# A transformer kernel: first self-attention in one block with float32r parts, further expert turns of 64 rows, exponents head by head, and another order of two loads

## The chip, the core and the metric

The kernel runs on one core of one Trainium2 chip. The measure is the device time of the whole program in microseconds; the median of several runs counts.

## What is computed

The reference takes x, 8 sequences of 64 rows of 512 (512 rows in all), and ctx, 8 times 1601 rows of 384, all float32. Six stages follow each other, each of them `x = x + stage(layernorm(x))`:

```python
x = x + _L0_xattn_ref(_layernorm(x), ctx_768, ...)   # 8 heads over the context
x = x + _L0_attn_ref(_layernorm(x), Wq, Wk, Wv)      # one head of 512, rotated q and k, mask tril(k=1)
x = x + _L0_ffn_ref(_layernorm(x), ...)              # 8 gated experts, 2 chosen per row, hidden 512
x = x + _L1_xattn_ref(_layernorm(x), ctx_768, ...)   # top-32 attention, FiLM, long convolution, feed-forward
x = x + _L1_attn_ref(_layernorm(x), Q, K, V, W)      # 16 heads of 64, causal
x = x + _L1_ffn_ref(_layernorm(x), ...)              # 8 GELU experts, 2 chosen per row, hidden 2048, a shared layer
```

The softmax of the two self-attentions is exact, and an expert works only for the rows that chose it.

## The kernel before

The 512 rows lie as four tiles of 128 (TT = 4), the 512 features as four chunks of 128 (KC = 4). A stage is one or several blocks; within a block each engine has its own program, and all order between engines is written out by hand with semaphores. At the end of a block all engines wait for each other. Loads go through SP's queue unless said otherwise. PE writes sums to PSUM, eight banks of 512 columns.

**First self-attention** (`self_attention_L0`, L610). A block holds only SP's six loads (L638 to L641). Then `norm_stage` (L133 to L167) normalises x on DVE and POOL, transposes it on PE and copies it to xt on ACT. Then comes the block of the work: PE multiplies Wq and Wk with xt in full precision (L667), four banks at a time, and K waits until DVE has multiplied Q by the tables (L698) and so freed the banks. The rotated halves are joined at L700 and L701. The values follow (L673), then the scores of each row tile (L680), mask (L704), maximum (L708), exponent with its sum (L726), reciprocal, a pass that divides (L714), the transposes (L685), the weighted values (L688) and the addition to x (L717). SP writes zeros to the two scratch tensors `sent` and `back` meanwhile (L651).

**Experts** (`experts`, L798), used for both mixtures. Each row's two chosen experts are found, and its normalised row is sent by POOL's indirect DMAs to `sent`, sorted by expert, each expert's rows padded to a multiple of 128. Then for each expert there is one fresh turn of 128 rows, and further turns if it has more (`turns`: a branch on the count, and a loop over k = 1 to 3 with a branch inside, on every engine). In a turn PE computes the hidden rows (`up`, L998) in NG groups of four chunks of 128, ACT applies bias and GELU for the second experts (L1252) and writes h; PE sums y from h and w2 (`down`, L985). In between it transposes the next 128 rows (L980), which ACT loads to e_xr (L1226; for the first time SP, L897, behind the weights of two experts) and copies to xg (L1230). DVE copies y (L1153) and ACT stores it to `back` (L1234). The last `down` of a turn stands after the first `up` of the next, and in a fresh turn a drain (L1014) follows it. It frees w2 for SP's load two experts on (L776 to L780). At the end POOL gathers each row's two results.

**End of the top-k attention** (`top_attention`). DVE picks the 32 best scores in passes of 8, ACT takes exponents, POOL subtracts (L2149), PE forms the mean attention (L1950) and weighs the context (L1965) for each of 8 batches. For the last batch PE first multiplies the value weights with the seven batches that are done (L1996); they come with ten small loads (`load_few`, L1769 to L1776), which SP issues after the filter weights (`load_film`, 4 MB, L1764), and these after the last scores.

**Second self-attention** (`self_attention_L1`). Projections with float32r: each float32 operand is cut into a high and a low part (ACT casts, L1457; DVE subtracts, L1510), and three products replace one in full precision (L1384). Then 16 units of 4 heads and 128 rows each. Per unit: scores on PE (L1405), on DVE scale and mask (L1529), maximum (L1532), subtraction (L1534), on ACT the exponent (L1479), on DVE sum (L1540), reciprocal, multiplication (L1544), on PE the transposes (L1414), on ACT a copy to pt (L1489), on PE the weighted values (L1425), on ACT a copy to yt (L1496). Every four units PE projects (L1434) and DVE adds to x (L1503).

## Time and profile before

| | us |
|---|---|
| Median of 3 runs | 1928.32 |
| The runs | 1927.71, 1928.32, 1939.1 |
| The profiled execution in all | 1944.16 |
| Its span (first to last instruction) | 1942.3 |

The page of the profile gives busy time by engine and line; the timeline gives operations in order with the engine's idle time before them and who ended it, in square brackets. An idle time matters only where PE, or whoever ends last, has it. The granted clock of TensorE was 0.944 of full speed on average. Matmuls in float32 stand as two records each, float32r ones and transposes as one.

### The profile page before, as it was taken

What the parts mean: (1) busy time and instruction counts of PE and PEld (TensorE: products, weight loads), DVE (VectorE), ACT (ScalarE), POOL (GpSimd) and SP (SyncE); (2) the same over time, 40 slices, a digit from 0 to 9 for tenths busy, and PEclk for the clock granted to TensorE, in tenths of its full rate; (3) what the DMA queues carried; (4) which work ended last, traced back from release to release, by engine and by line L of the source; (5) the groups of instructions that cost most, each with busy time, mean ns of one, the idle gap of its engine ahead of it and who ended that gap; (6) DMA issues with size and microseconds to landing.
All of it is one profiled execution on the core that took longest, in us unless ns stands there. A gap on an engine that the chain in (4) does not pass through costs nothing. (4 is left out here: it accounts for less than half of the span.)

```text
span 1942.3 us, 23742 instructions
## 1 busy us (share of the span) xinstructions
PE 1754.5 (90%) x8998; PEld 1350.7 (70%) x8998; DVE 981.5 (51%) x1490; ACT 573.9 (30%) x988; POOL 341.6 (18%) x294
## 2 busy tenths in 40 slices
PE   7899999999987889958999969797988899999994
PEld 3899999999953677723656547386775567777762
DVE  1667787686822434438899976644347310000003
ACT  4354443544410111113344412142433121111110
POOL 0432233312200010023454521100000010000002
PEclk9999999999998899978898989899989899999997
DMA  3332213322107346463444330700200565455802
GB/s 123 102 102 69 85 52 102 102 65 89 39 28 261 134 167 219 169 202 132 155 163 155 125 127 1 276 1 1 88 1 1 192 256 190 175 211 204 346 27 71
DMA packets 109978, 243.09 MB, mean 125 GB/s; under 512 B 13824, under 2 KB 43024, under 8 KB 105248
## 3 DMA queue, kind: packets, MB, share of 16 engines
q1 hardware_dynamic: 100672, 220.97, 32.1%
q10 hardware_dynamic: 6624, 12.06, 1.8%
q0 software_dynamic: 2560, 8.39, 1.3%
q8 instruction: 81, 1.33, 0.3%
q14 instruction: 41, 0.34, 0.1%
HBM read 221.48 MB, written 19.92 MB: 124 GB/s over the span
## 5 line engine op out<-in xcount | busy, mean ns | idle before, releaser
L998 PEld LDWEIGHTS e_ps<-e_xg,e_w 128*128 128x128 f32 x2304 | 269.0, 193 | 48.0 <-issue 45.6
L998 PE MATMUL e_ps<-e_xg,e_w 128*128 128x128 f32 x2304 | 272.4, 277 | 8.4 <-issue 4.4
L371 PE MATMUL x_s_ps<-x_cxt,x_qs 128*128 128x400 f32 (+1 forms) x1152 | 244.3, 357 | 10.0 <-POOL x_qs L344 5.9
L397 PE MATMUL x_o_ps<-x_cx,x_pt 128*128 128x386 f32 (+1 forms) x1248 | 230.3, 343 | 0.0
L985 PE MATMUL e_ps<-e_w,xt 128*128 128x512 f32 x480 | 221.0, 600 | 0.9 <-ACT xt L1252 0.6
L397 PEld LDWEIGHTS x_o_ps<-x_cx,x_pt 128*128 128x128 f32 (+1 forms) x1248 | 220.6, 190 | 1.4
L371 PEld LDWEIGHTS x_s_ps<-x_cxt,x_qs 128*128 128x128 f32 x1152 | 205.5, 191 | 11.2 <-issue 11.1
L1153 DVE COPY e_y<-e_ps 128x512 f32<-128x512 f32 x24 | 16.5, 688 | 340.1 <-PE e_ps L985 340.1
L1936 PE MATMUL x_s_ps<-x_cxt,x_qs 128*128 128x512 f32 (+1 forms) x384 | 142.7, 528 | 7.8 <-POOL x_qs L2132 5.8
L985 PEld LDWEIGHTS e_ps<-e_w,xt 128*128 128x128 f32 x480 | 86.6, 192 | 84.2 <-issue 82.2
L1252 ACT ACTIVATE xt<-e_ps,e_b 128x128 f32<-128x128 f32 x192 | 54.8, 369 | 282.1 <-PE e_ps L998 276.1
L1936 PEld LDWEIGHTS x_s_ps<-x_cxt,x_qs 128*128 128x128 f32 x384 | 68.6, 196 | 84.9 <-issue 79.0
L447 DVE TENSOR_TENSOR x_pt<-x_t_ps,x_pt 128x512 fp32r<-128x512 f32 (+1 forms) x128 | 74.7, 587 | 91.4 <-ACT x_pt L537 91.1
L537 ACT CAST x_pt<-x_t_ps 128x512 fp32r<-128x512 f32 (+1 forms) x128 | 64.6, 506 | 158.4 <-PE x_t_ps L383 157.4
L1284 POOL DMA_INDIRECT e_w<-back,m_row x16 | 16.5, 1032 | 497.1 <-ACTq L1270 492.8
L2203 DVE MAX8 x_best<-x_left 128x8 f32<-128x1601 f32 x48 | 87.8, 1829 | 1.7
L2205 DVE MATCH_REPLACE8 x_left<-x_best,x_left 128x1601 f32<-128x1601 f32 x48 | 86.9, 1811 | 0.0
L383 PE MATMUL x_t_ps<-ident,x_pr 128*128 128x128 f32 (+1 forms) x416 | 66.6, 274 | 2.0 <-DVE x_pt L447 2.0
L438 DVE TENSOR_REDUCE x_nmost<-x_s_ps 128x1 f32<-128x1600 f32 x32 | 58.4, 1825 | 14.4 <-PE x_s_ps L371 14.4
L513 ACT ACTIVATE x_pr<-x_s_ps,x_nmax 128x1600 f32<-128x1600 f32 x32 | 51.2, 1600 | 47.0 <-DVE x_nmax L440 47.0
L332 POOL TENSOR_TENSOR x_cx<-x,x_cx 128x1536 fp32r<-128x1536 f32 (+1 forms) x16 | 34.0, 2124 | 154.1 <-PE x_o_ps L397 144.8
L1950 PE MATMUL x_a_ps<-x_mean,x_sc 128*128 128x64 f32 (+1 forms) x416 | 56.3, 306 | 4.2 <-POOL x_sc L2149 4.2
(369 smaller groups left out, 2565.1 us busy)
## 6 DMA issues: line engine op xcount, KB each, us to landing
e_w<-in_L_ffn_W SPq DMA_DIRECT2D x16, 4096.0 KB, 16.3
x_cxt<-in_ctxT SPq DMA_DIRECT2D x8, 2401.5 KB, 8.6
x_cx<-in_ctx SPq DMA_DIRECT2D x8, 2304.0 KB
e_w<-in_L_ffn_gate_up_proj SPq DMA_DIRECT2D x8, 2048.0 KB, 11.1
x_stage<-in_ctxT SPq DMA_DIRECT2D x16, 768.0 KB, 4.4
x_stage<-in_ctx SPq DMA_DIRECT2D x16, 768.0 KB, 5.8
e_w<-in_L_ffn_down_proj SPq DMA_DIRECT2D x8, 1024.0 KB, 9.2
ff_w<-in_L_xattn_W SPq DMA_DIRECT2D x2, 4096.0 KB
```

The lines of the kernel that those rows point to most:

```text
L371: last = nc.tensor.matmul(s_ps[:, n, 0:b - a], qs[:, u % 2, p, c, :], cxt[:, q, c, a:b], start=(m + c == 0), stop=(m + c == len(PARTS) + C ...
L383: last = nc.tensor.transpose(t_ps[0:rows, g % 2, (t - a) * P:(t - a + 1) * P], pr[:, t * P:t * P + rows], ident[:, :])
L397: last = nc.tensor.matmul(o_ps[:, 0:WIDE], pt[0:rows, p, t, :], cx[0:rows, q, t, :], start=(t + m == 0), stop=(t + m == KT - 1 + len(PARTS ...
L438: nc.vector.reduce_max(nmost[:, u % 2:u % 2 + 1], s_ps[:, :, 0:400], AXIS.XY, negate=True).then_inc(most_ready, 1)
L447: nc.vector.tensor_tensor(pt[0:rows, 1, a:b, :], t_ps[0:rows, g % 2, 0:(b - a) * P].rearrange("p (t n) -> p t n", n=P), pt[0:rows, 0, a:b, ...
L537: nc.scalar.copy(pt[0:rows, 0, a:b, :], t_ps[0:rows, g % 2, 0:(b - a) * P].rearrange("p (t n) -> p t n", n=P)).then_inc(pth_ready, 1)
L985: last = nc.tensor.matmul(y_ps, h[:, c, :], w2[:, e % PAIR, c, :], start=(c == 0), stop=(c == HC - 1))
L998: last = nc.tensor.matmul(u_ps[:, g % 2, a * PER + n, :], w1[:, e % PAIR, m, a * hidden + c * P:a * hidden + (c + 1) * P], xg[:, m, :], st ...
L1936: last = nc.tensor.matmul(s_ps[:, lo:hi], qs[:, r, c, :], cxt[:, j, c, lo:hi], start=(c == 0), stop=(c == CC - 1))
L1950: last = nc.tensor.matmul(a_ps[0:rows, t * S:(t + 1) * S], sc[:, j, r, t * P:t * P + rows], mean[:, r, :], start=(r == 0), stop=(r == HALV ...
L2203: V.max(best[:, r, 8 * n:8 * n + 8], source).then_inc(steps, 1)
L2205: V.match_replace(left[:, r, :], best[:, r, 8 * n:8 * n + 8], source, TAKEN).then_inc(steps, 1)
```

## The change

Four parts. **A**: the first self-attention becomes one block: SP's loads, the norm and the work together. Wq, Wk, Wv and x are cut into float32r parts, and each projection is three products (`PARTS`); Q and K have four banks each. The weight tiles are taken in the order 0, 2, 1, 3, and DVE rotates in four turns of half a matrix. Two value tiles stand before the scores, two after. The pass that divides is gone: the reciprocal goes into the last addition. **B**: in the second experts a further turn has 64 rows (`MORE`): rows are the stationary side, the weights the moving one; GELU is applied on rows, the result transposed back. The bias is added by DVE from rows that two more loads per expert bring. A fresh turn ends with its own `down` groups and has no drain. In both mixtures the loop (third turn and later) now stands before the second turn. **C**: in the second self-attention ACT subtracts the maximum as its bias, head by head, and sums. **D**: `load_few` goes before `load_film`. The setting of lines that both versions share is left out here.

```diff
             @block.sync
             def _(sp):
-                for dst, name, s in ((wq, "L0_attn_Wq", in_q), (wk, "L0_attn_Wk", in_k), (wv, "L0_attn_Wv", in_v)):
-                    sp.dma_start(dst[:, :, :], w[name].rearrange("(c p) n -> p c n", p=P)).then_inc(s, 16)
-                sp.dma_start(cos[:, :, :], w["rope_cos"].rearrange("(c p) n -> p c n", p=P)).then_inc(in_tab, 16)
-                sp.dma_start(sin[:, :, :], w["rope_sin"].rearrange("(c p) n -> p c n", p=P)).then_inc(in_tab, 16)
-                sp.dma_start(mask[:, :], w["mask_L0"]).then_inc(in_tab, 16)
-
...
-            @block.sync
-            def _(sp):
+                for slot, name, s in ((0, "L0_attn_Wq", in_q), (1, "L0_attn_Wk", in_k)):
+                    sp.dma_start(wqk[:, slot, :, :], w[name].rearrange("(c p) n -> p c n", p=P)).then_inc(s, 16)
+                for a, name in enumerate(("rope_cos", "rope_sin")):
+                    sp.dma_start(tables[:, a, :, :], w[name].rearrange("(c p) n -> p c n", p=P)).then_inc(in_tab, 16)
...
+                for n in range(2 * KC):
+                    bank = (n // KC) * KC + ORDER[n % KC]
+                    for p, q in PARTS:
+                        if n == 0:
+                            pe.wait_ge((xh_ready, xl_ready)[q], TT)
+                        pe.wait_ge((wh_ready, wl_ready)[p], n + 1)
                         for c in range(KC):
...
+                            last = nc.tensor.matmul(ps[:, bank, :], part(n, p)[:, c, :], xs[:, q, c, :],
+                                                    start=(c == 0 and p + q == 0), stop=(c == KC - 1 and q == 1))
...
+                def value(t):
+                    for p, q in PARTS:
+                        pe.wait_ge((vh_ready, vl_ready)[q], KC)
+                        for c in range(KC):
+                            last = nc.tensor.matmul(ps[:, t, :], xs[:, p, c, t * P:(t + 1) * P], vs[:, q, c, :],
+                                                    start=(c == 0 and p + q == 0), stop=(c == KC - 1 and q == 1))
+                    last.then_inc(v_ready, 1)
+
+                pe.wait_ge(rot_ready, 4)
+                value(0)
+                value(1)
+                pe.wait_ge(rot_ready, 8)
                 for t in range(TT):
                     for c in range(KC):
...
+                        last = nc.tensor.matmul(ps[:, KC + t, 0:P], rot[:, 0, c, t * P:(t + 1) * P], rot[:, 1, c, t * P:(t + 1) * P],
                                                 start=(c == 0), stop=(c == KC - 1))
                     last.then_inc(s_ready, 1)
+                value(2)
+                value(3)
                 for t in range(TT):
-                    pe.wait_ge(norm_ready, t + 1)
-                    nc.tensor.transpose(qk_ps[:, t, 0:P], pr[:, t, :], ident[:, :]).then_inc(t_ready, 1)
+                    pe.wait_ge(exp_ready, t + 1)
+                    nc.tensor.transpose(ps[:, KC + t, P:2 * P], pr[:, t, :], ident[:, :]).then_inc(p_ready, 1)
...
+                norm.statistics(dve)
+                norm.rows(dve)
+                for t in range(TT):
+                    weight_low(t)
+                    dve.wait_ge(xh_ready, t + 1)
+                    here = xs[:, :, :, t * P:(t + 1) * P]
+                    V.tensor_tensor(here[:, 1, :, :], tps[:, t, :, :], here[:, 0, :, :].bitcast(F32), ALU.subtract).then_inc(xl_ready, 1)
+                for n in range(KC, 2 * KC):
+                    weight_low(n)
+                for c in range(KC):
+                    dve.wait_ge(vh_ready, c + 1)
+                    V.tensor_tensor(vs[:, 1, c, :], wv[:, c, :], vs[:, 0, c, :].bitcast(F32), ALU.subtract).then_inc(vl_ready, 1)
+                dve.wait_ge(in_tab, 32)
...
+                    for j in range(HALF):
+                        turn = a * HALF + j
+                        even, odd = ps[:, a * KC + j, :], ps[:, a * KC + HALF + j, :]
+                        cos, sin = tables[:, 0, j, :], tables[:, 1, j, :]
+                        dve.wait_ge(qk_ready, 2 * turn + 2)
+                        dve.wait_ge(rot_ready, 2 * turn)
+                        for n, (source, table) in enumerate(((even, cos), (odd, sin), (even, sin), (odd, cos))):
+                            V.tensor_tensor(tmp[:, n, :], source, table, ALU.mult).then_inc(prod_ready, 1)
+                        dve.wait_ge(prod_ready, 4 * turn + 2)
+                        V.tensor_tensor(rot[:, a, j, :], tmp[:, 0, :], tmp[:, 1, :], ALU.subtract).then_inc(rot_ready, 1)
+                        dve.wait_ge(prod_ready, 4 * turn + 4)
+                        V.tensor_tensor(rot[:, a, HALF + j, :], tmp[:, 2, :], tmp[:, 3, :], ALU.add).then_inc(rot_ready, 1)
...
                     dve.wait_ge(y_ready, t + 1)
-                    nc.vector.tensor_tensor(x[:, t, :], x[:, t, :], r_ps[:, t, :], ALU.add)
+                    V.scalar_tensor_tensor(x[:, t, :], ps[:, t, :], red[:, 2, t:t + 1], x[:, t, :], ALU.mult, ALU.add)
...
+                def weight_high(n):
+                    if n % KC == 0:
+                        act.wait_ge((in_q, in_k)[n // KC], 16)
+                    nc.scalar.copy(part(n, 0), tile(n)).then_inc(wh_ready, 1)
+
                 for t in range(TT):
+                    weight_high(t)
+                    act.wait_ge(t_ready, t + 1)
+                    nc.scalar.copy(xs[:, 0, :, t * P:(t + 1) * P], tps[:, t, :, :]).then_inc(xh_ready, 1)
+                for n in range(KC, 2 * KC):
...
                 for t in range(TT):
                     act.wait_ge(max_ready, t + 1)
                     nc.scalar.activation(pr[:, t, :], pr[:, t, :], ACT.Exp, bias=red[:, 0, t:t + 1],
...
+                    if t == 1:
+                        copy_value(3)
+                    act.wait_ge(p_ready, t + 1)
+                    nc.scalar.copy(pt[:, t, :], ps[:, KC + t, P:2 * P]).then_inc(pt_ready, 1)
 
...
+                sp.dma_start(self.b1_rows[half * S:(half + 1) * S, e % PAIR, :, :], bcast(self.up_rows[e, half], S)
+                             ).then_inc(self.rows_in[e % PAIR], 16)
         sp.dma_start(self.w2[:, e % PAIR, :, :], self.down_w[e].rearrange("(c p) n -> p c n", p=P)).then_inc(self.w2_in[e % PAIR], 16)
 
...
-                            engine.reg_add(register, register, 1)
+                    with engine.Fori(BLOCKS + 1, TOK // MORE) as k:
+                        with engine.If(k * MORE < tokens):
+                            one_more(e)
+                    one_more(e)
             return engine.snap(register, min_val=1, max_val=TURNS)
 
         with nc.Block() as block:
@@ -985,27 +1082,29 @@
...
+                def fresh_turn(e, t):
+                    pe.wait_ge(w1_in[e % PAIR], (e // PAIR + 1) * 16)
+                    pe.wait_ge(xg_ready, t + 1)
+                    one = up(e, t, 0)
+                    if e:
+                        one.then_inc(w1_free, 1)
+                    else:
+                        pe.wait_ge(b_ready, TT)
+                    one = up(e, t, 1)
+                    if e:
+                        one.then_inc(w2_free, 1)
+                        pe.wait_ge(y_ready, t)
+                    pe.wait_ge(w2_in[e % PAIR], (e // PAIR + 1) * 16)
+                    for g in range(NG):
+                        pe.wait_ge(h_ready, t * NG + (g + 1))
+                        last = down(e, g)
+                        if g + 2 < NG:
+                            up(e, t, g + 2)
+                        if g + 3 == NG:
+                            pe.wait_ge(x_in, (t + 1) * 16)
...
+                def more_turn(e, t, n):
+                    pe.wait_ge(xg_ready, t + 1)
+                    for p in range(2):
+                        for m in range(KC):
+                            for half in range(2):
+                                lo = half * S
+                                last = nc.tensor.matmul(ur_ps[lo:lo + S, p, :], xg[:, m, 0:S],
+                                                        w1[:, e % PAIR, m, (2 * p + half) * 512:(2 * p + half + 1) * 512],
+                                                        start=(m == 0), stop=(m == KC - 1))
+                        last.then_inc(up_ready, NG // 2)
+                    for p in range(2):
+                        pe.wait_ge(smooth, n * 2 + (p + 1))
+                        for c in range(KC):
+                            last = nc.tensor.transpose(ht_ps[:, p, c * P:(c + 1) * P], hr[:, p, c * P:(c + 1) * P], core.ident[:, :])
+                        last.then_inc(turned, 1)
+                        if p == 0:
+                            pe.wait_ge(x_in, (t + 1) * 16)
+                            turn_rows()
+                    pe.wait_ge(y_ready, t)
+                    for p in range(2):
+                        pe.wait_ge(h_ready, t * NG + (p + 1) * (NG // 2))
+                        for c in range(KC):
+                            for half in range(2):
+                                for q in range(2):
+                                    last = nc.tensor.matmul(y_ps[q * S:(q + 1) * S, 0:D // 2], h[:, p * KC + c, half * S:(half + 1) * S],
+                                                            w2[:, e % PAIR, (2 * p + half) * KC + c, q * (D // 2):(q + 1) * (D // 2)],
+                                                            start=(p + c + half == 0), stop=(p == 1 and c == KC - 1 and half == 1))
+                    last.then_inc(down_ready, 1)
+
+                if gated:
...
+                def more_turn(e, t, n):
+                    dve.wait_ge(rows_in[e % PAIR], (e // PAIR + 1) * 32)
+                    for p in range(2):
+                        dve.wait_ge(up_ready, t * NG + (p + 1) * (NG // 2))
+                        V.tensor_tensor(hr[:, p, :], ur_ps[:, p, :], weights.b1_rows[:, e % PAIR, p, :], ALU.add).then_inc(added, 1)
+                    for p in range(2):
+                        dve.wait_ge(turned, n * 2 + (p + 1))
+                        V.tensor_copy(h[:, p * KC:(p + 1) * KC, :], ht_ps[:, p, :].rearrange("p (c n) -> p c n", n=P)).then_inc(h_ready, NG // 2)
+                    dve.wait_ge(down_ready, t + 1)
+                    dve.wait_ge(y_out, (t + 1) * 16)
+                    V.tensor_copy(y[:, 0:D // 2], y_ps[:, 0:D // 2]).then_inc(y_ready, 1)
+
...
+                def more_turn(e, t, n, row):
+                    act.wait_ge(x_ready, t + 1)
+                    load_rows(row + 1)
+                    for p in range(2):
+                        act.wait_ge(added, n * 2 + (p + 1))
+                        nc.scalar.activation(hr[:, p, :], hr[:, p, :], ACT.Gelu).then_inc(smooth, 1)
+                    copy_rows(t + 1)
+                    act.wait_ge(y_ready, t + 1)
+                    act.dma_start(back[bass.ds(row * MORE, S), :].rearrange("r (h n) -> h r n", h=2), y[:, 0:D // 2]).then_inc(y_out, 16)
 
                 act.sem_inc(y_out, 16)
                 copy_rows(0, first_ps)
...
                     nc.scalar.copy(v[:, t, half * 512:(half + 1) * 512], ps[:, n % 8, :]).then_inc(p_used, 1)
                 def exponent(u):
-                    act.wait_ge(low_ready, u + 1)
-                    nc.scalar.activation(pr[:, u % AHEAD, :, :], pr[:, u % AHEAD, :, :], ACT.Exp).then_inc(exp_ready, 1)
+                    act.wait_ge(max_ready, u + 1)
+                    for k in range(G):
+                        one = pr[:, u % AHEAD, k, :]
+                        last = nc.scalar.activation(one, one, ACT.Exp, bias=red[:, u % AHEAD, 0, k:k + 1],
+                                                    accum_out=red[:, u % AHEAD, 1, k:k + 1])
+                    last.then_inc(exp_ready, 1)
 
...
                                                    mask[:, :].unsqueeze(1).broadcast_to([P, G, P]), ALU.mult, ALU.add).then_inc(sm_ready, 1)
                     dve.wait_ge(sm_ready, u + 1)
-                    nc.vector.reduce_max(red[:, k, 0, :], pr[:, k, :, :], AXIS.X).then_inc(max_ready, 1)
-                    dve.wait_ge(max_ready, u + 1)
-                    nc.vector.tensor_tensor(pr[:, k, :, :], pr[:, k, :, :], red[:, k, 0, :].unsqueeze(2).broadcast_to([P, G, P]),
-                                            ALU.subtract).then_inc(low_ready, 1)
+                    nc.vector.reduce_max(red[:, k, 0, :], pr[:, k, :, :], AXIS.X, negate=True).then_inc(max_ready, 1)
 
                 def normal(u):
                     k = u % AHEAD
                     dve.wait_ge(exp_ready, u + 1)
-                    nc.vector.reduce_sum(red[:, k, 1, :], pr[:, k, :, :], AXIS.X).then_inc(sum_ready, 1)
-                    dve.wait_ge(sum_ready, u + 1)
                     nc.vector.reciprocal(red[:, k, 2, :], red[:, k, 1, :]).then_inc(inv_ready, 1)
                     dve.wait_ge(inv_ready, u + 1)
                     nc.vector.tensor_tensor(pr[:, k, :, :], pr[:, k, :, :], red[:, k, 2, :].unsqueeze(2).broadcast_to([P, G, P]),
...
                     if b + 3 == B:
+                        sp.wait_ge(qs_ready, B * HALVES)
+                        mix.load_few(sp)
                         sp.wait_ge(s_ready, B * HALVES)
                         mix.load_film(sp)
-                        sp.wait_ge(qs_ready, B * HALVES)
-                        mix.load_few(sp)
```

## Rows read from the trace of the kernel before

**Rows 1.** The page: busy by engine; chain by engine; one costliest group.

```profile
PE 1754.5 (90%) x8998; PEld 1350.7 (70%) x8998; DVE 981.5 (51%) x1490; ACT 573.9 (30%) x988; POOL 341.6 (18%) x294
...
PE 18%; DMA 1%; DVE 1%; POOL 0%; issue 0%; DVEq 0%; ACT 0%; ACTq 0%
...
L1153 DVE COPY e_y<-e_ps 128x512 f32<-128x512 f32 x24 | 16.5, 688 | 340.1 <-PE e_ps L985 340.1
```

**Rows 2.** Timeline (start us, us, operation), PE in the second experts' turns.

```profile
1615.61 0.60 PE L980 MATMUL e_ps<-ident,e_xr 128*128 128x128 f32 x4
...
1623.06 3.60 PE L985 MATMUL e_ps<-e_w,xt 128*128 128x512 f32 x8
...
1644.58 0.60 PE L980 MATMUL e_ps<-ident,e_xr 128*128 128x128 f32 x4
...
1673.04 0.60 PE L980 MATMUL e_ps<-ident,e_xr 128*128 128x128 f32 x4
```

**Rows 3.** Timeline of the first self-attention.

```profile
582.75 0.37 SPq L638 DMA_DIRECT2D s_wq<-in_L_attn_Wq  x1
...
588.17 3.22 PE L156 MATMUL n_tps<-ident 128*128 128x128 f32 x14 [7.68 <-PEq L634]
...
596.15 13.97 PE L667 MATMUL s_qk_ps<-xt,s_wq 128*128 128x512 f32 x32 [1.84 <-PEq L54]
...
614.99 16.72 PE L667 MATMUL s_qk_ps<-xt,s_wk 128*128 128x512 f32 x32 [4.87 <-DVE s_tmp L698]
...
651.65 1.12 PE L685 MATMUL s_qk_ps<-ident,s_pr 128*128 128x128 f32 x4 [2.64 <-DVE s_pr L714]
...
657.29 0.69 DVE L717 TENSOR_TENSOR x<-x,s_r_ps 128x512 f32<-128x512 f32 x1 [0.17 <-PE s_r_ps L688]
```

**Rows 4.** Timeline of the second self-attention's loop: two projections.

```profile
1463.48 7.13 PE L1434 MATMUL s_ps<-s_wz,s_yt 128*128 128x512 f32 x16
...
1484.24 7.13 PE L1434 MATMUL s_ps<-s_wz,s_yt 128*128 128x512 f32 x16
```

**Rows 5.** Groups of instructions: busy us, mean ns, idle before; records that price the parts.

```profile
L1384 PE MATMUL s_ps<-s_xs,s_ws 128*128 128x512 f32 x192 | 45.3, 399 | 3.2 <-DVE s_ws L1510 3.2
...
L1534 DVE TENSOR_TENSOR s_pr<-s_pr,s_red 128x512 f32<-128x512 f32 x16 | 11.1, 692 | 0.6
...
L1540 DVE TENSOR_REDUCE s_red<-s_pr 128x4 f32<-128x512 f32 x16 | 10.9, 678 | 0.0
...
L1479 ACT ACTIVATE s_pr<-s_pr 128x512 f32<-128x512 f32 x16 | 10.1, 629 | 4.0 <-DVE s_pr L1534 3.9
...
L726 ACT ACTIVATE s_pr<-s_pr,s_red 128x128 f32<-128x128 f32 x4 | 1.6, 390 | 3.5 <-DVE s_red L708 3.5
```

**Rows 6.** Timeline of the end of the top-k attention.

```profile
1135.55 11.15 PE L1996 MATMUL x_s_ps<-x_ct,x_qp 128*128 128x448 f32 x24 [9.44 <-DMA x_qp<-in_dft_inverse]
...
1141.11 3.02 POOL L2149 TENSOR_TENSOR x_sc<-x_sc,x_left 128x1601 f32<-128x1601 f32 x1
...
1146.54 5.70 PE L1950 MATMUL x_a_ps<-x_mean,x_sc 128*128 128x64 f32 x52
```

**Rows 7.** Timeline: matmuls with 64 stationary columns, from three stages.

```profile
1153.29 4.73 PE L1965 MATMUL x_e_ps<-x_cx,x_at 128*64 128x384 f32 x26 [1.05 <-ACT x_at L2066]
...
1219.50 1.93 PE L2377 MATMUL mx_ps<-mx_spec,x_qp 128*64 128x512 f32 x4 [1.34 <-DVE mx_spec L2405]
...
1515.03 1.83 PE L1425 MATMUL s_ps<-s_pt,s_v 128*64 128x128 f32 x16
```

**Rows 8.** Timeline: the second experts' first turned rows and what follows.

```profile
1585.39 0.66 PE L980 MATMUL e_ps<-ident,e_xr 128*128 128x128 f32 x4 [2.38 <-DMA e_xr<-sent]
1585.89 5.29 PE L985 MATMUL e_ps<-e_w,xt 128*128 128x512 f32 x8
```

**Rows 9.** Busy by engine in two stretches; then granted clock, DMA share, GB/s.

```profile
616.00:620.00 4.00, 4.00 (x6) 1.66 (x5) 1.24 (x2) 0.00 (x0) 0.00 (x0) 0.50 0.91 338
1620.00:1640.00 20.00, 19.74 (x115) 14.30 (x115) 0.69 (x1) 3.43 (x12) 0.00 (x0) 1.00 0.95 362
```

## What the change will do to the time

> **What bounds the kernel.** I read the page first. Over a span of 1942.3 us PE is busy 90% and DVE 51%; the named part of the chain that ended last is 18% PE, almost all of it the second experts [rows 1]. So a microsecond counts where PE works longer or waits, and the other engines count only where PE waits for them. Then I read the four places that the diff touches in the timeline, each for the operation that ends last there.
>
> In the second experts PE sets the pace and nothing else does. The 24 copies of y are 24 turns, 12 for each block of experts [rows 1]. From one group of turned rows to the next a turn takes 28.97 us (1615.61 to 1644.58), or 28.46 us (1644.58 to 1673.04) where no drain stands in it [rows 2].
>
> In the first self-attention PE works on full-precision matmuls, which the trace records in two instructions each: 32 records of 512 columns take 13.97 us, and the same work for K takes 16.72 us after PE had sat 4.87 us waiting for DVE [rows 3]. Its norm starts at 588.17, though SP was already at the stage's loads at 582.75: the closing barrier of the block of loads holds all engines until SP has issued them.
>
> In the second self-attention's loop of 16 units, one projection follows the last by 20.76 us (1463.48 to 1484.24) [rows 4]. Its own 7.13 us are PE's. The rest is paced by DVE: five passes of 0.68 to 0.69 us and a reciprocal of 0.18 us, some 3.6 us a unit, two of the passes being the subtraction (L1534) and the sum (L1540) [rows 5].
>
> At the end of the top-k attention PE waits 9.44 us for the last of ten small loads, works 11.15 us at 1135.55, and only at 1146.54 begins the mean attention, though POOL's last subtraction was over at 1144.1 [rows 6].
>
> **A, first self-attention.** Removed: two block boundaries and the wait behind SP, 588.17 - 582.75 = 5.4 us. Norm, split and projections now overlap: first matmul before at 596.15, so 590.7 by the shift, but it also waits for four row tiles and the first weight tile to be cut in two parts on ACT (eight passes of 512, about 0.63 us each as L1479 has it [rows 5]) and on DVE. I put it at 592.5. Each of the 96 projection matmuls for Q and K (8 tiles, 3 part products, 4 chunks) is one record; the same form at L1384 takes 45.3 / 192 = 0.236 us [rows 5], so 22.7 us, plus 1.5 us for a cold start after the splits: 616.7. DVE's rotation, now six passes of 0.69 us per half matrix, hides behind them, and only the last, 3.9 us, ends after (620.6). It is hidden by the first two value tiles, 24 x 0.236 = 5.7 us, to 622.4. If that cover were gone, it would cost 3.9 us. Scores stay full precision, 32 records of 128 columns, some 3.7 us, to 626.1. The last two value tiles, 5.7 us, to 631.8, cover mask, maximum and exponent. The tail from the first transpose to the end took 658.0 - 651.65 = 6.3 us [rows 3]. The normalising pass has gone from in front of it (reciprocals and multiplications are folded into the final add), a last copy of V has come in, 0.6 us; I leave it at 5.0. End at 636.8 for 658.0: **-21**. Bounds: with every matmul at its row and no cold start -25, with PE waiting for the splits at each of the first four tiles -16. The two 4 MB zero stores need until about the end of the projections, as before, and 15 us of slack lie behind them. SP issues the same loads, the value weights now after the tables; V is needed last.
>
> **B, second experts.** The routing of the reference on its own inputs gives 135, 134, 119, 172, 77, 84, 119 and 184 rows: four experts have more than 128, none more than 192. So there are four further turns, as now, each of 64 rows. Upwards such a turn is 16 matmuls (32 records) with 64 stationary and 512 moving columns, alternating between the two halves of PSUM's partitions; downwards 32 matmuls (64 records) of 256 moving columns, alternating too. Does the array run the two halves at once? Three rows say yes. The weighted values at L1965, also alternating, take 4.73 / 26 = 0.182 us a record at 384 columns [rows 7]. L985's 128-wide stationary needs 3.60 / 8 = 0.45 us a record at 512 columns [rows 2], or 0.34 scaled to 384. L2377, 64 wide in one half only, needs 1.93 / 4 = 0.48 us: it is the alternating that helps, not the width [rows 7]. Scaled by columns, up is 32 x 0.243 = 7.8 us. Down would be 64 x 0.121; L1425 shows 1.83 / 16 = 0.114 at only 128 moving columns [rows 7], a floor near it, so I take 0.13: 8.3 us. Eight more transposes and the four of the next rows are 1.3 us. Gelu and bias now stand between up and down: PE waits for an add (0.69, as L1534), a Gelu (0.63, as L1479) and semaphores after the second half, less the transposes that fill it, 1.0 us. Sum 18.4 for 28.46, -10.1 a turn, **-40.2** for four. Bounds: both halves perfectly parallel (half of 0.43, floor 0.114) 16.5 us, or -48; no overlap at all 29.9 us, or +5.8.
>
> The Trainium skill (TensorEngine Tiling, Performance Considerations and Key Properties) promises up to a factor of two for a stationary side of 64 or less, but adds that a change of tiling mode drains the engine. By the first alone the turn would be 16.5 us. In the trace PE goes from L1425 to the next form with no visible gap, so the drain is small here.
>
> The fresh turn keeps its work and loses the software pipelining across turns. Nothing new is exposed: down(2) and down(3), 6.9 us, cover the last Gelu (1.14 us) and the copy of the next rows, and the next up(0) and up(1) cover the copy of y. ACT's store now waits for that copy ahead of the next Gelu, which is due a whole up(0) later. The drain goes: 7 x 0.51 = -3.6 us (28.97 - 28.46). On the other side, two bias-row loads of 0.5 MB per expert join SP's queue. The first two experts' lie in front of e_xr, for which PE already waits 2.38 us [rows 8]; 1.05 MB at 362 GB/s [rows 9] are +2.9 us, and the following down was slow after the wait (5.29 us for 3.60 [rows 8]), so +0.9. Five false loop passes instead of two behind each fresh turn: PE has 3.4 us of queued work over them; I add 1.0 in all. The Trainium skill (Advanced Engine Details and Errata, Control Flow Timing) puts a compare-and-branch near 0.1 us, by which all of it stays covered. B together **-39**. The first experts get the same loop order and nothing else: 0.
>
> **C, exponents.** DVE loses 0.69 + 0.68 us a unit and is left with 2.2. ACT gets four exponents of 128 with their sums in place of one of 512: L726, the same form, 1.6 / 4 = 0.40 us each [rows 5], 1.6 for 0.63, plus the copies of pt and yt, 512 columns each, so 0.6 as L1479 [rows 5]: 2.8 us a unit. ACT becomes the pacer, at 2.8 for 3.6. Of four units one is covered by the projection, three gain 0.8 to 1.0: -2.6 us per projection, **-10.5** in all. Bounds: ACT's waits eat half, -4; PE's own work is the pace (scores, turning and weighing are some 2.4 us a unit), -13.
>
> **D, order of loads.** The small loads no longer stand behind 4 MB of filter weights and behind the last scores. Values can start when the last-but-one batch's result is copied, near 1126.5, and be over by 1136. The mean attention then waits for POOL's subtraction. It needs ACT's exponent after DVE's last pick, both unmoved, and starts near 1142.6 for 1146.54: -3.9 us. What is late next is PE's clock: it will have idled 6 us, as before L1996: 11.15 us [rows 6] for 24 records that need 9.0 (0.43 us x 448 / 512 each). A shorter stretch follows here, so +1.4. **-2.5**; bounds -5 and 0.
>
> **Sum.** -21 - 39 - 10.5 - 2.5 = **-73**. The profiled execution took 1944.16 us in all (span 1942.3), so 1871 there. It was 15.8 us above the median of the runs; against the median of 1928.32 the same terms give **1855**.
>
> **Rivals.**
> - *No overlap of the two halves* (PSUM or weight loads serialise them): a further turn is 29.9 us, B is +7, total 1901. Against: L1965 beside L2377. For: no row has the 256-column form.
> - *ACT holds the exponents up*: each waits for its maximum, C is 0, total 1866. For: ACT then works without slack. Against: AHEAD is 3, DVE is done 1.4 us a unit earlier.
> - *Half clock in the further turns*: the granted clock stood at 0.50 between 616 and 620 us, behind the 4.87 us gap before K [rows 9]. If it fell in each further turn, 16.1 us double: +64, total 1919. Against: the planned gap is 1.0 us, and gaps of 0.8 us in the second self-attention slow nothing.
> - *Slower than before: weights arrive late.* Single-turn experts give the next 8.9 MB their 28.5 us plus the 7 before the first down. At the 362 GB/s of [rows 9] they land in 25 us. To lose 73 + 19 us over six loads each must land 15 us late, in some 47 us: it decides from 190 GB/s downwards. No row shows so little while weights are under way.
>
> **Numbers.** Forecast 0.72 (1838 to 1874, by the bounds taken together), no overlap 0.12, exponents 0.08, half clock 0.05, late weights 0.03. Range 1832 to 1890: it holds the forecast and the exponents, and reaches towards a partial overlap. About 1% is what a measurement of this kernel tells from no change, so faster means below 1909: 0.92; same 0.05; slower 0.03.
>
> **What would show it.** A: no PE gap over 1 us between Q and K, next norm some 21 us sooner. B: further turns of 18 us, records of 256 columns at 0.13 us; PE's wait for e_xr near 5 us. C: projections 18.2 us apart, DVE idle before each reciprocal. D: the mean attention starts when POOL ends. The forecast is wrong first if the 256-column records take over 0.2 us.

## The result and the profile after

The changed kernel takes 1872.88 us in the median (runs of 1871.78, 1871.80, 1873.95 and 1880.78 us), against 1929.97 us for the kernel before on the same chip: a ratio of 0.972, with a 95% interval of 0.968 to 0.976. The median fell by 57 us where 73 were forecast. The profiled execution of after stands at its median (1871.78 us); that of before stood some 15 us above its own. The median lies in the stated range (1832 to 1890), 1 us inside the upper end of the forecast's own stretch (1838 to 1874). So the forecast of 1871 against the profiled execution met its mark almost exactly and the 1855 against the median was 18 us too low, and the first question is what those 15 us were.

First the page of the changed kernel: busy time by engine, the queues that fetch instructions, the chain by engine, and the group that answers to the copies of y in [rows 1].

```profile
span 1870.0 us, 23575 instructions
...
PE 1695.7 (91%) x8822; PEld 1307.9 (70%) x8822; DVE 980.1 (52%) x1498; ACT 582.0 (31%) x1056; POOL 340.1 (18%) x294
...
q8 instruction: 90, 1.47, 0.3%
q14 instruction: 47, 0.39, 0.1%
...
PE 16%; DMA 2%; DVE 1%; issue 1%; POOL 0%; ACTq 0%; ACT 0%; DVEq 0%
...
L1310 DVE COPY e_y<-e_ps 128x512 f32<-128x512 f32 x20 | 13.7, 686 | 239.7 <-PE e_ps L1082 239.7
```

PE is still the bound, with 59 us less of work. The copies of 512 columns are 20 and no longer 24: the other four are those of the further turns. In the chain, DMA has come up from 1% to 2% and "issue", waits that no profiled instruction ends, from 0% to 1% [rows 1]. Most of what the forecast missed lies in those two.

Read stage by stage (from the first start of one line to that of the next), the profiles tell more than the totals. "Again" is a second profile of before; the other columns are experiments told below.

| stage, us | before | again | e1 | after | e3 | e8 | e9 |
|---|---|---|---|---|---|---|---|
| to the first experts' router (A ends in it) | 664.0 | 665.9 | 645.6 | 643.0 | 641.1 | 643.5 | 643.3 |
| first experts, to their first gather | 170.5 | 166.9 | 164.2 | 174.7 | 162.8 | 163.4 | 165.1 |
| to the last pick of the top-k attention | 299.2 | 291.8 | 291.0 | 292.1 | 289.0 | 291.9 | 293.7 |
| last pick to filter stage (D) | 33.2 | 31.6 | 35.3 | 31.5 | 35.3 | 35.2 | 35.3 |
| to the scores of the second self-attention | 269.2 | 268.1 | 269.1 | 268.2 | 269.0 | 269.1 | 269.1 |
| scores to the last addition to x (C) | 88.6 | 88.6 | 79.4 | 75.8 | 85.7 | 81.0 | 74.4 |
| second experts, to the end (B) | 417.6 | 415.9 | 417.7 | 384.7 | 389.6 | 366.3 | 366.8 |

**Part A**, in the timeline of after (start, us, operation, the engine's idle time before it):

```profile
592.01 24.54 PE L687 MATMUL s_ps<-s_xs,s_qks 128*128 128x512 f32 x96 [2.57 <-ACT s_xs L776]
...
616.39 5.60 PE L695 MATMUL s_ps<-s_vs,s_xs 128*128 128x512 f32 x24
...
621.83 3.73 PE L705 MATMUL s_ps<-s_rot 128*128 128x128 f32 x32
...
625.32 5.70 PE L695 MATMUL s_ps<-s_vs,s_xs 128*128 128x512 f32 x24
...
632.79 3.31 DVE L764 SCALAR_TENSOR_TENSOR x<-s_ps,s_red,x 128x512 f32<-128x512 f32 x4 [5.86 <-PE s_ps L716]
```

Where [rows 3] have 13.97 us, a gap of 4.87 and 16.72 us, there are 96 records in one piece, and every boundary lies within 0.8 us of the one forecast.

**Part B.** PE in the second experts: the wait for the first turned rows and the slow records behind it, a further turn, then a place where one expert's fresh turn follows another's.

```profile
1553.90 1.11 PE L1077 MATMUL e_ps<-ident,e_xr 128*128 128x128 f32 x4 [8.58 <-DMA e_xr<-sent]
1554.81 9.54 PE L1082 MATMUL e_ps<-e_w,xt 128*128 128x512 f32 x16
...
1609.13 7.09 PE L1159 MATMUL e_ps<-e_w,e_xg 128*64 128x512 f32 x32
...
1618.26 7.13 PE L1177 MATMUL e_ps<-e_w,xt 128*64 128x256 f32 x64
1625.32 7.41 PE L1090 MATMUL e_ps<-e_xg,e_w 128*128 128x128 f32 x64
...
1647.02 7.03 PE L1082 MATMUL e_ps<-e_w,xt 128*128 128x512 f32 x16
1655.31 7.41 PE L1090 MATMUL e_ps<-e_xg,e_w 128*128 128x128 f32 x64 [1.26 <-issue]
```

A further turn is 1625.32 - 1609.13 = 16.2 us. The wait for e_xr is 8.58 us and no longer 2.38, with 9.54 us for 7.03 behind it [rows 8]. At 1655.31 stands a gap that before did not have.

**Part C.** The four projections, for [rows 4]:

```profile
1430.70 7.13 PE L1621 MATMUL s_ps<-s_wz,s_yt 128*128 128x512 f32 x16
...
1448.52 7.13 PE L1621 MATMUL s_ps<-s_wz,s_yt 128*128 128x512 f32 x16
...
1466.34 7.13 PE L1621 MATMUL s_ps<-s_wz,s_yt 128*128 128x512 f32 x16
...
1478.16 7.13 PE L1621 MATMUL s_ps<-s_wz,s_yt 128*128 128x512 f32 x16 [0.67 <-ACT s_yt L1687]
```

The first three stand 17.82 us apart, for 20.76; the last, which has less work in front of it, follows after 11.82 us, for 12.54. Between two of them PE has no gap (its busy time is the first number behind the length, ACT's the fourth):

```profile
1448.52:1466.34 17.82, 17.82 (x97) 11.87 (x96) 9.31 (x18) 10.73 (x41) 0.00 (x0) 1.00 0.00 1
```

### The profile page after: what moved, and what is told of

Its sections match the earlier page's. It is cut to its first block and busy times, and to the rows that moved or that the text cites. A ratio compares the mean times of both kernels' runs of the same rounds, so it can differ in the third digit from the quotient of the medians.

```text
span 1870.0 us, 23575 instructions
## 1 busy us (share of the span) xinstructions
PE 1695.7 (91%) x8822; PEld 1307.9 (70%) x8822; DVE 980.1 (52%) x1498; ACT 582.0 (31%) x1056; POOL 340.1 (18%) x294
## 5 line engine op out<-in xcount | busy, mean ns | idle before, releaser
L1090 PEld LDWEIGHTS e_ps<-e_xg,e_w 128*128 128x128 f32 x1792 | 208.8, 194 | 43.9 <-issue 42.1
L1090 PE MATMUL e_ps<-e_xg,e_w 128*128 128x128 f32 x1792 | 212.4, 278 | 16.3 <-issue 14.6
L371 PEld LDWEIGHTS x_s_ps<-x_cxt,x_qs 128*128 128x128 f32 x1152 | 206.2, 192 | 11.2 <-issue 11.1
L1082 PE MATMUL e_ps<-e_w,xt 128*128 128x512 f32 x352 | 163.4, 606 | 0.9 <-ACT xt L1427 0.6
L1082 PEld LDWEIGHTS e_ps<-e_w,xt 128*128 128x128 f32 x352 | 64.7, 195 | 65.3 <-issue 64.2
L1427 ACT ACTIVATE xt<-e_ps,e_b 128x128 f32<-128x128 f32 x128 | 36.4, 369 | 193.5 <-PE e_ps L1090 187.5
L1320 DVE TENSOR_SCALAR e_tmp<-e_ps,e_b 128x128 f32<-128x128 f32 x48 | 14.6, 346 | 88.3 <-PE e_ps L1090 84.8
```

Of the source, the lines that this page charges most:

```text
L371: last = nc.tensor.matmul(s_ps[:, n, 0:b - a], qs[:, u % 2, p, c, :], cxt[:, q, c, a:b], start=(m + c == 0), stop=(m + c == len(PARTS) + C ...
L1082: last = nc.tensor.matmul(y_ps, h[:, c, :], w2[:, e % PAIR, c, :], start=(c == 0), stop=(c == HC - 1))
L1090: last = nc.tensor.matmul(u_ps[:, g % 2, a * PER + n, :], w1[:, e % PAIR, m, a * hidden + c * P:a * hidden + (c + 1) * P], xg[:, m, :], st ...
```

## The experiments

Each ratio is taken against runs of the kernel before on the same chip. Their medians were 1928.2 us (e1 to e4), 1928.8 (e5 to e8) and 1932.7 (e9 to e11), so medians of different groups compare to a few us only. e5, e6, e7 and e11 ran once; their totals say little, their stages more.

**e1: A, C and D without B.** The experts' functions of before stand in a kernel that has the rest of the change.

> The kernel before with parts A, C and D, and without B (experts unchanged). Theory: the profiles gave A 20.7 us, C 12.8, D 1.7, so 35 us less than before, about 1893 for a median of 1928; the first experts, which lost 4 us in the changed kernel, take as long as before again (170.5 us to the gather), so their loss came with B's loops. The picks of the top-k attention (first to last pick) took 247 us in the profile of before and 239 in the one after, with the same code: if that was a matter of the one execution, they take about 239 here too, and the profile of before stood some 8 us too high there. Rival: the first experts lose their 4 us here as well (an effect of A, whose stores of zeros or loads reach into them); then 1897, and 174.7 us to the gather.

Measured: 1897.0 us, ratio 0.981 (0.975 to 0.987), so -31 us; with B it is -57. That is the total that the rival named, but not for its reason: the first experts took 164.2 us, not its 174.7 and not the expected 170.5 either. The loss there comes with B's loops, and with nothing of A. The picks took about as long as in after (241 us from the first to the last, for 239, and 247 in the first profile of before).

**e5: the kernel before, profiled again.**

> The kernel before, profiled once more. Its first profile stood 15.8 us above the median of its runs, and PE was at half clock there from 925 to 942 us in the midst of the first picks of the top-k attention, while it was busy. Theory: stages with the same code differ by what the clock does in them, so this profile nears 1928, with the first experts at 162 to 165 us (logits to gather) instead of 170.5 and the picks at 239 to 241 instead of 247. Rival: the difference sits in A, B, C or D themselves; then these two stages read 170 and 247 again.

Measured: 1930.6 us in all, span 1928.8, 13.5 us less than the first profile. The table shows where: 3.6 us in the first experts, 7.4 up to the last pick, 1.6 behind it, 1.1 in the filter stages and 1.7 in the second experts, less 1.9 us more ahead of A. A itself and C read the same, and the code of all these stages was the same in both. So it is nothing that the change removes. Two waits of the first profile show where most of it came from:

```profile
804.42 5.46 PE L998 MATMUL e_ps<-e_xg,e_w 128*128 128x128 f32 x32 [2.15 <-DMA e_w<-in_L_ffn_gate_up_proj]
...
954.43 1.83 DVE L2203 MAX8 x_best<-x_sc 128x8 f32<-128x1601 f32 x1 [7.32 <-POOL x_sc L2139]
```

In the first experts PE waited for weights, 1.08 and 2.15 us, and ran slower behind the second wait (5.46 us for 3.73); the second profile has one such wait, of 1.81 us, and that of e10, with the same code there, none: 165.0 us. In the picks it is the clock: in the first profile PE was at a granted clock of 0.52 from 925 to 942 us, the next scores came late, and DVE, which sets the pace there, waited 7.32 us. In the second profile PE was at 0.50 from 1105 to 1120 us instead, busy 13.95 us, and DVE had no such wait.

**e3: the old loop in both experts.**

```diff
-                    with engine.Fori(BLOCKS + 1, TOK // MORE) as k:
+                    with engine.Fori(BLOCKS, TOK // MORE) as k:
                         with engine.If(k * MORE < tokens):
                             one_more(e)
-                    one_more(e)
```

> The changed kernel with the loop as before in both experts: one copy of the further turn in a loop from the second turn on, not a loop and then a second copy. Theory: the first experts lost 4 us because three copies of a turn per expert are more code to fetch than two, and PE sat idle in the middle of a row of matmuls (1.89, 1.30 and 4.14 us, ended by nothing the profile shows); with the old loop these waits go, -4 us, 1868. In the second experts the gap of 1.26 us between the last down of a turn and the next expert's first up also shrinks if the length of the jump over the further turns makes it. Rival: the code's form changes nothing, the idle times are the weights' (the sum of first experts stays 174.7 us), 1872; then the extra false pass in front of each further turn could cost up to 1 us.

Measured: 1870.0 us, 0.968 (0.961 to 0.975). Below are PE's longest waits of the kind "issue" in the first experts (us in total, times, longest), and the packets of instruction fetches there (packets, MB, share), first of after, then of e3:

```profile
PE e_ps L1090 <- issue: 9.2, 10, 4.1
...
q8 instruction: 16, 0.26, 0.6%
q14 instruction: 9, 0.07, 0.1%
```

```profile
PE e_ps L1089 <- issue: 1.8, 7, 0.3
...
q8 instruction: 12, 0.20, 0.5%
q14 instruction: 6, 0.05, 0.1%
```

With three copies of a turn per expert instead of two, 25 packets of code are fetched and not 18, and PE sits idle 7.4 us longer, once in the midst of a row of equal matmuls. It is so in every profile: the five others with the new loop have 25 or 26 packets and 9.1 to 10.2 us of such waits in this stage, e1, e8 and e9 with the old one 17 or 18 packets and 1.8 to 2.8 us.

The rows of after:

```profile
698.15 2.17 PE L1090 MATMUL e_ps<-e_xg,e_w 128*128 128x128 f32 x18
702.21 1.72 PE L1090 MATMUL e_ps<-e_xg,e_w 128*128 128x128 f32 x14 [1.89 <-issue]
...
786.88 6.19 PE L1090 MATMUL e_ps<-e_xg,e_w 128*128 128x128 f32 x32 [4.14 <-issue]
```

Behind the longest of them the clock has fallen (6.19 us for 3.81), another 2.4. The stage is 162.8 us for 174.7. The waits and the slower matmuls behind the longest make some 10 of these 12 us. The expectation of 4 us was too small, since it was read against a before that had been slow. The Trainium skill (Runtime: NRT & Kernel Launch, Instruction fetch mechanics) says that a taken branch to a place outside the fetched window stalls until that page is there; the packet counts and the idle time agree with it. No run shows the size of the window.

In the second experts the old loop removes the gap between fresh turns (28.46 us apart), but puts 2.65, 2.73 and 2.82 us of idle time behind a further turn, where the loop's five false passes now follow it. Whether the passes or the way back in the loop cost that, no run separates:

```profile
1578.60 8.92 PE L1089 MATMUL e_ps<-e_xg,e_w 128*128 128x128 f32 x64 [2.65 <-issue]
...
1617.90 7.13 PE L1176 MATMUL e_ps<-e_w,xt 128*64 128x256 f32 x64
1627.75 7.41 PE L1089 MATMUL e_ps<-e_xg,e_w 128*128 128x128 f32 x64 [2.73 <-issue]
```

The clock falls behind two of the three (8.92 and 9.03 us for 7.41), and the stage becomes 389.6 us for 384.7. So the new loop looks right there (in one profile of each) and is wrong in the first experts.

**e4: all ups before the downs in a fresh turn.** The hidden groups 2 and 3 go to banks 0 and 1.

```diff
+                    for g in range(2, NG):
+                        up(e, t, g)
                     for g in range(NG):
                         pe.wait_ge(h_ready, t * NG + (g + 1))
                         last = down(e, g)
-                        if g + 2 < NG:
-                            up(e, t, g + 2)
-                        if g + 3 == NG:
+                        if g == 1:
```

> The changed kernel; in a fresh turn of the second experts the hidden groups 2 and 3 go to banks 0 and 1, all four ups stand before the four downs, so no down waits for a Gelu that has just been issued. Theory: the gap of 1.26 us at the four places where one expert's fresh turn follows another's comes because PE's sequencer stood at the wait for the last Gelu and could not run ahead to the branch; it shrinks to the 0.3 us that before had: -4 to -5 us, 1868. Rival: the gap is the jump over the skipped further turns itself, whatever stood ahead of it: it stays at 1.26 us, 1872.

Measured: 1871.8 us, 0.970 (0.965 to 0.976), for the expected 1868. Where one fresh turn follows another the turned rows stand 28.69 to 28.84 us apart, not 29.93 to 29.99, and from 1616.6 us on, where both profiles stand at the same place, this one gains 5.6 us to the last turned rows (205.3 us for 210.9); its profile ends 6.0 us below after's. Its median shows nothing of that: its four runs spread over 15 us. The gap thus depends both on what stands queued in front of the jump (this run) and on how far the jump goes (e3). Which share is the wait for the Gelu and which the fetch stays open.

**e2: e_xr ahead of expert 1's weights.**

```diff
-                weights.load_up(sp, 1)
-                weights.load_down(sp, 1)
                 sp.wait_ge(rows_sent, SENT)
                 sp.dma_start(xr[:, :], sent[P:2 * P, :]).then_inc(x_in, 16)
+                weights.load_up(sp, 1)
+                weights.load_down(sp, 1)
```

> The changed kernel; in the second experts SP loads e_xr before the weights of expert 1 instead of behind them. Theory: the wait of 8.58 us at L1077 and the slow records behind it (9.54 us for 7.03) come from the queue ahead of e_xr, 1.05 MB of bias rows included: both go, -9 to -11 us, and e_xr lands in 2 to 4 us after its issue; 1862. The weights of expert 1 then start some 35 us later than now, but have until about 1575 to land 9.4 MB: covered. Rival 1: e_xr waits for the sends of POOL, not for the queue: its issue stays at 52 us after the stage's start, and of 8.6 us at most 5 go. Rival 2: the later weights of expert 1 are late for its first turn: a new wait of up to 10 us, no change in all.

Measured: 1869.9 us, 0.969 (0.964 to 0.974), for the expected 1862; its profile runs within 0.2 us of after's up to the second experts and ends 11.2 us sooner (1858.8 for 1870.0). By the medians it is 3 us, with runs spread from 1861 to 1877, so the gain is shown by the profile and not by the medians. e_xr is issued at 1530.74 and not at 1539.56, it lands 2.6 us after its issue and not 14.3, and there is no wait left in front of the first turned rows:

```profile
1530.74 0.33 SPq L995 DMA_DIRECT2D e_xr<-sent  x1
...
1545.31 0.60 PE L1081 MATMUL e_ps<-ident,e_xr 128*128 128x128 f32 x4
1545.74 7.03 PE L1086 MATMUL e_ps<-e_w,xt 128*128 128x512 f32 x16
```

**e11: only the bias rows go behind e_xr.**

```diff
                 sp.dma_start(xr[:, :], sent[P:2 * P, :]).then_inc(x_in, 16)
+                weights.load_bias_rows(sp, 0)
+                weights.load_bias_rows(sp, 1)
```

> The changed kernel; in the second experts the bias rows of experts 0 and 1 (four loads, 1.05 MB) are issued behind e_xr, the weights stay ahead of it. Theory: while such a load runs, the trace shows 153 to 234 and 213 to 282 GB/s with the DMA engines full, for 385 otherwise, so these rows cost 5 to 6 us and not the 2.9 of their bytes: from the last addition to x to the first turned rows 68.6 - 5.5 = 63 us, PE's wait for e_xr 3 us for 8.6. Rival: bytes alone count: 65.7 us and a wait of 5.7 us.

Measured (one run, 1883.4 us): from the last addition to x to the first turned rows 63.0 us for 68.6. That is the 5.5 us of the theory, not the 2.9 of the bytes. The wait is 4.56 us, not the expected 3, because PE was ready for these rows 1.6 us sooner than in after. The run's total is high mainly for another reason, the clock in the second self-attention (85.8 us from scores to last addition, for 75.8). What a load of bias rows looks like in stretches of after (third number from the end the granted clock, then the DMA engines' share and GB/s):

```profile
1506.00:1508.00 2.00, 2.00 (x6) 0.93 (x5) 0.00 (x0) 0.00 (x0) 0.00 (x0) 1.00 1.12 377
1508.00:1510.00 2.00, 2.00 (x6) 0.80 (x6) 0.00 (x0) 0.00 (x0) 0.00 (x0) 1.00 0.94 153
1510.00:1512.00 2.00, 2.00 (x15) 1.59 (x14) 0.92 (x5) 0.15 (x1) 0.00 (x0) 1.00 1.02 234
1512.00:1514.00 2.00, 2.00 (x6) 0.87 (x5) 1.93 (x8) 0.00 (x0) 0.00 (x0) 1.00 1.04 387
```

In the second and third row the engines are as full as ever and move about half as much. In e1, which has no such loads, no stretch between 1506 and 1542 us moves less than 351 GB/s. The load reads the same 4 KB for each of 64 partitions; that this repetition is what makes it slow was not tested by itself.

**e6: no alternation between the halves.** In a further turn `half` (up) and `q` (down) become outer loops.

```diff
-                        for m in range(KC):
-                            for half in range(2):
+                        for half in range(2):
+                            for m in range(KC):
...
+                    for q in range(2):
                         for p in range(2):
...
-                                for q in range(2):
```

> The changed kernel; in a further turn of the second experts the matmuls of one half of PSUM's partitions stand before those of the other, in up (16 of them) and in down (32), and do not alternate. Theory: 64 wide matmuls run two at a time only where neighbours go to different halves. Then a record of 512 columns takes 0.43 us and not 0.22, one of 256 columns 0.21 and not 0.11: up 13.8 us for 7.1, down 13.7 us for 7.1, a further turn 29.5 us for 16.2, and the time rises by 53 us to about 1925. Rival: a narrow stationary side is fast by itself, in whatever order: 1872.

```profile
1627.81 8.97 PE L1159 MATMUL e_ps<-e_w,e_xg 128*64 128x512 f32 x32
...
1638.81 13.22 PE L1177 MATMUL e_ps<-e_w,xt 128*64 128x256 f32 x64
```

Measured: 1914.8 us (one run), the second experts 414.5 us for 384.7, and a further turn 24.2 us, not the expected 29.5. Down, in two blocks of 32 records, takes 0.207 us a record and not 0.111, about half of what 512 columns take without overlap (0.43): no overlap at all. Up, in four blocks of 8 records, takes 0.28 us, neither the 0.22 of alternation nor that 0.43. So it is the order that makes the rate, but neighbours need not alternate one by one. Why blocks of 8 keep most of it was not found.

**e7: the wait in front of the first turning filled.**

```diff
                     if u + 2 < U:
                         scores(u + 2)
+                    if u == 0:
+                        for n in range(IDLE):
+                            nc.tensor.transpose(ps[:, 7, 0:P], ident[:, :], ident[:, :])
```

> The changed kernel; in the second self-attention 14 transposes of the identity into a bank that is not used (bank 7) stand in the wait of 2.19 us in front of the first turning of a unit. Theory: it is this wait that lets PE's clock fall: after it the same four transposes take 1.11 us and no longer 0.66, and a unit 4.94 us and no longer 2.69, until the clock returns, which cost three profiles 21.2, 24.8 and 31.1 us from the first scores to the first projection. Filled, the clock stays and this stretch is about 18.5 us: -3 to -10 us. Rival: the clock falls for the gaps before (0.68 and 0.31 us), or whatever is put there; then 21 to 31 us again, plus up to 2 us where the filling comes out too long.

The same place in after, then in e7:

```profile
1414.87 0.66 PE L1601 MATMUL s_ps<-ident,s_pr 128*128 128x128 f32 x4 [2.19 <-DVE s_pr L1730]
...
1417.00 1.11 PE L1601 MATMUL s_ps<-ident,s_pr 128*128 128x128 f32 x4 [0.39 <-DVE s_pr L1730]
...
1421.03 0.66 PE L1601 MATMUL s_ps<-ident,s_pr 128*128 128x128 f32 x4
```

```profile
1410.66 1.75 PE L1632 MATMUL s_ps<-ident 128*128 128x128 f32 x14
1412.92 0.66 PE L1601 MATMUL s_ps<-ident,s_pr 128*128 128x128 f32 x4 [0.51 <-DVE s_pr L1733]
...
1415.06 0.65 PE L1601 MATMUL s_ps<-ident,s_pr 128*128 128x128 f32 x4 [0.39 <-DVE s_pr L1733]
```

Measured (one run): 1866.6 us. Behind the open wait four transposes take 1.11 us, half clock, and 0.66 again later; behind the filled one they never leave 0.66. From the first scores to the first projection it is 19.8 us, for 21.2 to 31.1 in the eight profiles with part C and an open wait, and 74.4 us from the scores to the last addition where those had 75.8 to 85.8. The expected 18.5 us was not reached. Against the profile of after the stage gains only 1.4 us, since the clock there fell for 3 us only; e9 has the same 19.8 and 74.4 us. The rival, that the clock would fall for the shorter gaps before, is ruled out by both.

**e10: D alone,** in the kernel before.

```diff
                     if b + 3 == B:
+                        sp.wait_ge(qs_ready, B * HALVES)
+                        mix.load_few(sp)
                         sp.wait_ge(s_ready, B * HALVES)
                         mix.load_film(sp)
-                        sp.wait_ge(qs_ready, B * HALVES)
-                        mix.load_few(sp)
```

> The kernel before with part D alone (the small loads before the filter weights). Theory: in the second profile of before PE did not wait for those loads at all: its own matmuls, at half clock, took until 1124.9, and the mean attention began as soon as they and POOL were done. The 9.44 us of the first profile were slack in front of the same end. So no change: 1928, within 5 us, and from the last pick to the filter stage 31.5 or 35.3 us by the clock. Rival: -2.5 us or more, 1925, with PE waiting for POOL instead of the loads.

Measured: 1929.2 us over ten runs, a ratio of 0.9985 (0.9959 to 1.001).

```profile
1116.44 9.26 PE L1996 MATMUL x_s_ps<-x_ct,x_qp 128*128 128x448 f32 x24 [0.50 <-ACT x_ct L2076]
...
1129.36 3.02 POOL L2149 TENSOR_TENSOR x_sc<-x_sc,x_left 128x1601 f32<-128x1601 f32 x1 [0.28 <-ACT x_left L2060]
...
1132.43 10.95 PE L1950 MATMUL x_a_ps<-x_mean,x_sc 128*128 128x64 f32 x52 [6.74 <-POOL x_sc L2149]
```

The values start early and the mean attention starts when POOL is done, at 1132.4, as the forecast had it. But PE has idled 6.74 us, its clock is down (0.50 from 1132 to 1148), the matmuls take 10.95 us for the 5.70 of [rows 6], and the next group (L1965) 7.30 us for the 4.73 of [rows 7]. From the last pick to the filter stage it is 37.0 us, for 33.2 and 31.6 without D.

**e8 and e9: put together.** e8 has the old loop in the first experts and e2's and e4's edits in the second; e9 also fills the wait.

```diff
-                    with engine.Fori(BLOCKS + 1, TOK // MORE) as k:
+                    with engine.Fori(1 if gated else BLOCKS + 1, TOK // MORE) as k:
                         with engine.If(k * MORE < tokens):
                             one_more(e)
-                    one_more(e)
+                    if not gated:
+                        one_more(e)
```

> The changed kernel with three edits: the old loop in the first experts only, e_xr ahead of expert 1's weights in the second experts, and the four ups before the four downs there. Theory, by stage lengths of the runs of each alone: first experts 163 us from logits to gather (174.7), second experts' wait for e_xr gone (-11.2), fresh turns 28.7 us apart for 29.95 where a fresh one follows (-5.7). Sum -28, about 1844. Rival: the 12 us of the first experts came from a clock that fell at another place in that one execution and only the issue waits go, 7 us: 1849 and a spread as wide as now.

> The changed kernel with the three edits of the combination and the filled wait in the second self-attention. Theory: the stage lengths add up: 163 us in the first experts, 57.5 us to the first turned rows of the second, and 19.8 us from the first scores to the first projection of the second self-attention (26.4 in the profile without the filling, 21.2 in that of the changed kernel). So 2 to 7 us below the combination's 1849, about 1845, and more alike from run to run than its 1838 to 1867. Rival: the clock that is kept there falls a little later (the same total of time at half clock per run, 186 to 209 us so far); then 1849 and the same spread.

Measured: e8 1849.5 us, 0.956 (0.952 to 0.960); e9 1843.8 us, 0.953 (0.950 to 0.957), 29 us below the changed kernel by the medians. Both beat both kernels. The stages of the experts add up as expected; e8's total is 5 us above its expected 1844, at the number of its rival, because its profile has 5.2 us more than after in the second self-attention and 3.7 us more behind the last pick, and not because the first experts gained less (163.4 us, 163 expected). The filling saves 6.6 us in its stage (74.4 for 81.0), and the difference of the two medians is of that size, though their intervals overlap. e9's six runs lie between 1836 and 1852 us, e8's four between 1838 and 1867.

## Why the prediction was right and where it was not

**A, right:** 21.0 us to the router, -21 forecast. No run has A alone, but its stage stands apart in every profile: 641.1 to 645.6 us with A, 664.0 to 665.9 without.

**B, right in kind, -32.9 for -39, with four terms mis-sized.**
- The further turn is 16.2 us, not 18.4: -12.3 each, -49 in place of -40.2. Scaling [rows 7] by columns was too careful. A record of 512 columns takes 7.09 / 32 = 0.22 us (0.243 forecast) and one of 256 columns 7.13 / 64 = 0.111 (0.13), close to a factor of two against the 0.43 and 0.207 without overlap; so 16.5 us, the better bound, was the right end to take. The Trainium skill (TensorEngine Tiling, Performance Considerations and Key Properties) promises up to that factor, and the trace agrees (1.95 and 1.86); of the drain that it names for a change of tiling mode nothing is to be seen, since L1159 starts at 1564.28 where L1082 ends.
- The loads of bias rows were priced by their bytes, at +2.9 us, and the records behind the wait at +0.9. To the first turned rows it was 68.6 us for 60.7, +7.9, and e11 puts 5.6 of them on the rows' slow loads; the other 2.3 stay open. The slow records came to +0.8.
- The step "five false loop passes; PE has 3.4 us of queued work over them; 1.0 in all", and with it "nothing new is exposed", fell. The passes run only for the four experts with more than 128 rows; for the others the branch skips the whole loop. Yet PE sits idle 1.20 to 1.27 us at the four places where one expert's fresh turn follows another's, with no pass between, and 1.30 us in front of the last expert's further turn, while the same five passes cost nothing in front of the other three. That is 6.3 us at five places, and e3 and e4 tie the four to the longer jump and to what is queued before it. The fresh turn itself is 28.66 us (1580.47 to 1609.13), so of the 3.6 us for drains 2.2 came.
- The tail was left out. The last copy of y to the first gather takes 5.8 us for 3.2: the last store now has two pieces per row and lies between the two. +2.5. That the pieces are the cause was not tested.

Together -49 + 7.9 + 0.8 + 6.3 - 2.2 + 2.5 = -34.

**The first experts, wrong at "the same loop order and nothing else: 0".** This is the step that failed. The same words in the diff meant another copy of the turn for each expert. It costs about 10 us: 174.2 to 175.0 us in the six profiles with the new loop, 162.8 to 165.1 in five with the old one, e10 with before's own code among them. The two profiles of before, at 170.5 and 166.9, had lost 1.8 to 5 us to late weights (e5). The runs show more packets of code fetched and PE idle with nothing else to wait for; that the one causes the other is the reading that fits, and not shown by itself. In the profiled totals the error was hidden, because the before profile had that stage slow, and the picks too.

**C, right with a wrong reason, and only if the clock holds.** 17.82 us between projections for 18.2. ACT was to be the pacer, at 2.8 us a unit. Its four exponents and two copies do take 4 x 0.39 + 2 x 0.58 = 2.7 us, but it is busy only 10.73 of the 17.82 us. PE is busy all of them: it needs 2.69 us a unit at full clock, not the 2.4 I had given it, and with the projection that is the whole distance. So the bound that the prediction put aside, PE's own work, is what sets the pace. In the stage, C is worth 88.6 - 75.8 = 12.8 us in after's profile; in other runs of the same code it was 9.2, 7.6 or 2.9, and 14.2 with the wait filled. In every profile 6.6 us of the gain lie between the first and the last projection; the rest lies in front of the first, where the clock decides. The rival of the exponents did not come about.

**D, right in mechanism, its gain not found.** In e10 the mean attention starts 8.9 us after the last pick, for 12.8 in the first profile of before: the -3.9 of the forecast. But the cold start was put at 1.4 us and is 5.25 in e10's mean attention and 2.6 in the group behind it. From the last pick to the filter stage the profiles with D read 31.5 to 37.0 us, the two without it 31.6 and 33.2. The median of D alone can't decide between 0 and -2.5: its interval reaches from -8 to +2 us. And the 9.44 us of [rows 6] were not typical: in the second profile of before PE's own work ran until 1124.9 us and it never waited for those loads.

**The median.** I took the 15.8 us between profile and median for a constant beside the terms. They were mostly 13.5 us of stages that ran slower that once. So the match of 1871 was luck: the profiles differ by 72.3 us for the 73 forecast, but only because 7.1 us in the picks, 1.0 in the filter stages (both with unchanged code) and 2.3 more in C made up for 6.1 missing in B, 4.2 in the first experts and 0.8 in D. With typical stages the sum is -21 (A), +4 to +10 (first experts), 0 (D), -8 (C, mean of eight profiles), -31 to -33 (B): -50 to -58, and 57 were measured.

Of the rivals none came true. No half clock stood in the further turns, no weights came late in the second experts, and the halves did overlap. The border for late weights was misworked: 28.5 + 7 + 15 us are 50.5 us, by which 8.9 MB need 176 GB/s, not 47 us and 190.

## What to carry to other kernels

Where a program branches on data, count the copies of the code that lie between the branch and its target, on every engine and in every stage that shares the helper: one copy more cost 10 us here, with no instruction of work added. A small load that was issued behind large ones landed 14.3 us after its issue, and 2.6 us when issued ahead of them, so send it first. And before a profile's waits are priced, take a second profile: a wait that exists in only one of them, or a gap that makes PE's clock fall, is worth something else than its length.

## What the runs showed of the hardware

- While loads that repeat one DRAM row over 64 partitions run, stretches of 2 us move 153 to 282 GB/s with all DMA engines busy, where the weights around them move about 385 (after); taking them out of the way of e_xr gained 5.6 us for 1.05 MB (e11).
- Two 64-wide streams of matmuls into different halves of PSUM's partitions run almost fully together when they alternate (after: 0.111 us a record of 256 columns), partly in blocks of 8 records (e6: 0.28 us for 0.22, at 512 columns), not at all in blocks of 32 (e6: 0.207 at 256 columns).
- Where the same code took different time in different profiles, PE's clock was the largest cause found: the second self-attention took 75.8 to 85.8 us from its scores on. A wait of 2.19 us was followed there by 3 to 27 us at half clock, depending on the run, and 1.75 us of transposes of the identity in it kept the clock at full (e7, e9).
- With three copies of a turn in the code instead of two, 25 or 26 packets of instructions were fetched in the first experts for 17 or 18, and PE sat idle 9.1 to 10.2 us, for 1.8 to 2.8, with nothing recorded that it waited for.
